# Quad 0, the identity taps and layer 3's rows in the prologue of a four-layer conditioned residual kernel

## The reference

```python
x = x + conv1d(x, W0, K=9, groups=4, pad=4) + (c @ cw.T)[:, :, None] + fside[None, :, None]
for n in (1, 2, 3):
    h = gelu(c @ W0n + b0n); h = gelu(h @ W1n + b1n)
    att = softmax(h @ W2n + b2n)                     # 8 experts per sample
    agg_w = einsum('bk,koi->boi', att, Wn)           # a 64x64 matrix per sample
    agg_b = att @ bias_kn
    x = x + einsum('boi,bih->boh', agg_w, x) + agg_b[:, :, None]
```

## Time and profile before

| | |
|---|---|
| median of 3 runs | 321.65 us (321.52 to 324.29) |
| the profiled execution | 323.18 us, its span 321.3 us |
| PE busy | 309.9 us, 96% of the span |
| DVE busy | 262.4 us, 82% |
| ACT busy | 228.2 us, 71% |
| POOL busy | 129.4 us, 40% |
| DMA | 104.53 MB, 325 GB/s over the span |

### The profile page before, as it was taken

The page is one execution under the profiler, slowest core; times in us unless marked ns, Lnnn a source line. Parts: engine busy times, 40 slices in busy tenths (PEclk is TensorE's granted clock), DMA queues, the critical chain, the costliest instruction groups (busy, mean ns, idle before and its releaser), DMA issues.

```text
span 321.3 us, 6082 instructions
## 1 busy us (share of the span) xinstructions
PE 309.9 (96%) x1474; PEld 251.8 (78%) x1474; DVE 262.4 (82%) x290; ACT 228.2 (71%) x346; POOL 129.4 (40%) x271
## 2 busy tenths in 40 slices
PE   8787999999999999999999999999999999999993
PEld 8556878888888888888888888888888888888872
DVE  5664788889887889888889888898888888987883
ACT  5544677777777788776777777887777777778663
POOL 5510397454444333444433444434444333344400
PEclk9998899999999999999999999999999999999999
DMA  7787366999999999899999999999999999996687
GB/s 230 218 234 281 134 222 212 370 365 364 348 340 342 372 337 373 337 365 360 363 380 340 354 341 359 340 373 336 361 370 353 370 344 368 344 363 280 266 329 274
DMA packets 30946, 104.53 MB, mean 325 GB/s; under 512 B 3428, under 2 KB 4708, under 8 KB 23113
## 3 DMA queue, kind: packets, MB, share of 16 engines
q1 hardware_dynamic: 30938, 104.43, 88.0%
HBM read 36.26 MB, written 33.55 MB: 217 GB/s over the span
## 4 chain that ended last, share of the span: by engine, by line
PE 91%; DMA 3%; SPq 2%; ACT 1%; DVE 1%; issue 0%; DVEq 0%
PE bank L409 54%; PE bank L451 9%; PE bank L453 9%; PE bank L452 9%; PE bank L417 4%; DMA x_sb<-in_x 3%; PE bank L537 2%; SPq L283 2%; PE bank L459 1%; ACT x_hi L628 1%; PE bank L508 1%; PE bank L465 0%; DVE att L837 0%; PE bank L475 0%; PE bank L485 0%
## 5 line engine op out<-in xcount | busy, mean ns | idle before, releaser
L635 ACT ACTIVATE conv_sb<-bank 128x512 f32<-128x512 f32 x128 | 76.2, 596 | 62.9 <-PE bank L409 59.0
L355 POOL COPY a_diag<-table 64x64 f32 (+1 forms) x128 | 49.7, 388 | 132.2 <-PE bank L417 112.6
L762 DVE TENSOR_TENSOR x_lo<-x_sb,x_hi 128x2064 fp32r<-128x2064 f32 x31 | 71.5, 2308 | 24.5 <-ACT x_hi L628 23.3
L365 POOL COPY a_dup<-table 64x128 f32 (+1 forms) x128 | 70.9, 554 | 34.4 <-ACT table L680 16.9
L409 PE MATMUL bank<-x_hi,toep_hi 128*128 128x512 f32 x256 | 84.3, 411 | 0.1
L409 PE MATMUL bank<-x_lo,toep_hi 128*128 128x512 f32 x256 | 80.7, 397 | 0.0
L409 PE MATMUL bank<-x_hi,toep_lo 128*128 128x512 f32 x256 | 80.5, 395 | 0.0
L779 DVE TENSOR_TENSOR ybuf<-ybuf 128x1024 fp32r<-128x1024 f32 x62 | 77.1, 1244 | 1.1
L628 ACT ACTIVATE x_hi<-x_sb 128x2064 fp32r<-128x2064 f32 x32 | 61.7, 1928 | 11.3 <-DMA x_sb<-in_x 11.0
L655 ACT ACTIVATE out_sb<-bank,beta 128x512 f32<-128x512 f32 x93 | 63.4, 684 | 5.0 <-DMA out<-out_sb 1.8
L409 PEld LDWEIGHTS bank<-x_hi,toep_lo 128*128 128x128 f32 x256 | 48.3, 189 | 12.1
(11 more groups left out here) (95 smaller groups left out, 167.0 us busy)
## 6 DMA issues: line engine op xcount, KB each, us to landing
x_sb<-in_x SPq DMA_DIRECT2D x32, 1032.0 KB, 7.8
ybuf<-conv_sb SPq DMA_DIRECT2D x128, 256.0 KB, 5.0
out<-out_sb SPq DMA_DIRECT2D x29, 1024.0 KB, 7.9
out<-out_sb SPq DMA_DIRECT2D x8, 256.0 KB, 2.5
out_sb<-conv_sb SPq DMA_DIRECT2D x8, 128.0 KB
out<-x_sb SPq DMA_DIRECT2D x4, 256.0 KB, 3.4
x_sb<-in_toep SPq DMA_DIRECT2D x1, 640.0 KB, 6.1
early<-in_mixrow SPq DMA_DIRECT2D x1, 390.0 KB
```

The costliest lines, as they stand in the source:

```text
L355: nc.gpsimd.tensor_copy(a3_diag[rows, par, :, C * h + NH * e:C * h + NH * e + NH], table[0][C * e:C * e + C, here, h, :]).then_inc(comp_in, 1)
L365: nc.gpsimd.tensor_copy(a21_dup[rows, par, :, :, NH * e:NH * e + NH], table[1][C * e:C * e + C, here, h, :].unsqueeze(2).to_broadcast([C, ...
L635: nc.scalar.activation(conv_sb[:, par, g, :], conv_ps[g % banks][:, :], ACT.Copy).then_inc(conv_out, 1)
L762: nc.vector.tensor_tensor(x_lo[:, par].rearrange("p g s j -> p (g s j)"), x_sb[:, par].rearrange("p g s j -> p (g s j)"), x_hi[:, par].rea ...
```

## The change

The identity is added only in the columns where it isn't zero, in two instructions (for each of the two tap offsets d, the half of the phase columns that it occupies). Quad 0 is loaded in two transfers, and its high part is made in two instructions and its low part in three. ScalarE issues the four transfers of layer 3's rows, ahead of its first GELU. The first bias product moves behind two groups of the convolution of quad 0, the first bias transpose behind table bank 8, and the orders of ScalarE and VectorE are rewritten around them.

```diff
@@ SP @@
-            sp.wait_ge(rows3_zero, 1)
-            for i in range(RT):
-                n = C * C // RT
-                sp.dma_start(mrow[0][32 * i:32 * i + K + 1], own_h[0:K + 1, n * i:n * i + n]).then_inc(rows3_in, 16)
-            load(0, 0)
+            n = G // 2 * S * JX
+            sp.dma_start(x_sb[:, 0, 0:G // 2]..., x_h[0:128, 0:n]).then_inc(x0_first, 16)
+            sp.dma_start(x_sb[:, 0, G // 2:]..., x_h[0:128, n:]).then_inc(x_in[0], 16)
@@ GpSimd @@
-            nc.gpsimd.tensor_tensor(taps, taps, eyes.to_broadcast([128, 2, G, 128]), ALU.add).then_inc(toep_set, 1)
+            taps, eyes = (t.rearrange("p d g (m h) -> p d g m h", h=QP) for t in
+                          (taps, eye_tap.rearrange("p (d o m) -> p d o m", d=2, o=1)))
+            for d in range(2):
+                h = slice(QP // 2 * d, QP // 2 * d + QP // 2)
+                nc.gpsimd.tensor_tensor(taps[:, d, :, :, h], taps[:, d, :, :, h],
+                                        eyes[:, d, :, :, h].to_broadcast([128, G, 2 * CG, QP // 2]), ALU.add).then_inc(toep_set, 1)
@@ TensorE @@
-            bias_products(0)
             pe.wait_ge(toep_hi_set, 1)
             pe.wait_ge(toep_lo_set, 1)
             taken(BANKS.index(0))
             conv(0, 0, 0, banks=2)
             taken(BANKS.index(1))
+            pe.wait_ge(xlo_first, 2)
+            conv(0, 0, 1, banks=2)
+            bias_products(0)
+            pe.wait_ge(xhi_set, 1)
             pe.wait_ge(xlo_set, 1)
-            for g in range(1, G):
-                conv(0, 0, g, banks=2)
+            conv(0, 0, 2, banks=2)
+            conv(0, 0, 3, banks=2)
+            tables(8)
             bias_turn(0)
-            for t in (8, 9, 10):
-                tables(t)
+            tables(9)
+            tables(10)
             bias_products(1)
@@ ScalarE @@
+            act.wait_ge(rows3_zero, 1)
+            for i in range(RT):
+                n = C * C // RT
+                nc.scalar.dma_start(mrow[0][32 * i:32 * i + K + 1], own_h[0:K + 1, n * i:n * i + n]).then_inc(rows3_in, 16)
             for n in range(NL):
                 act.wait_ge(hid1_ps, n + 1)
...
-            act.wait_ge(toep_set, 1)
+            act.wait_ge(toep_set, 2)
...
-            x_high(0, 0, 0)
-            for t in ACT_TAKES:
-                if t < TG:
-                    table_bank(t)
+            for there, g, done in ((x0_first, slice(0, G // 2), xhi_first), (x_in[0], slice(G // 2, G), xhi_set)):
+                act.wait_ge(there, 16)
+                nc.scalar.activation(x_hi[:, 0, g], x_sb[:, 0, g], ACT.Copy).then_inc(done, 1)
+            table_bank(0)
             conv_copy(0, 0, 0, 0, banks=2)
+            table_bank(2)
             conv_copy(0, 0, 0, 1, banks=2)
+            table_bank(4)
+            table_bank(6)
             conv_copy(0, 0, 0, 2, banks=2)
-            x_high(1, 0, 1)
-            vcol_copy(0)
             conv_copy(0, 0, 0, 3, banks=2)
             table_bank(8)
+            vcol_copy(0)
+            x_high(1, 0, 1)
@@ VectorE @@
             table_bank(3)
+            dve.wait_ge(xhi_first, 1)
+            x_low_part(slice(0, 1)).then_inc(xlo_first, 1)
+            x_low_part(slice(1, 2)).then_inc(xlo_first, 1)
             table_bank(5)
             dve.wait_ge(xhi_set, 1)
-            for g, done in ((slice(0, 1), xlo_first), (slice(1, G), xlo_set)):
-                nc.vector.tensor_tensor(x_lo[:, 0, g], ...).then_inc(done, 1)
+            x_low_part(slice(2, G)).then_inc(xlo_set, 1)
             table_bank(7)
             bias_sum(0)
-            x_low(1, 1)
             table_bank(9)
             bias_sum(1)
             table_bank(11)
+            x_low(1, 1)
             table_bank(13)
             table_bank(15)
             bias_sum(2)
             x_low(2, 0)
             y_low(0, 0, 0)
+            mix_low(0, 0)
             y_low(0, 0, 1)
-            mix_low(0, 0)
```

More of the change, by code:

```diff
@@ L189, in cond_resid_kernel @@
         x_in = [sem("x_in0"), sem("x_in1")]
+        x0_first, xhi_first = sem("x0_first"), sem("xhi_first")
         stored = [sem("stored0"), sem("stored1")]
@@ L266, in _ @@
             sp.dma_start(ident[:], kept_h).then_inc(kept_in, 16)
-            sp.wait_ge(rows3_zero, 1)
-            for i in range(RT):
-                n = C * C // RT
-                sp.dma_start(mrow[0][32 * i:32 * i + K + 1], own_h[0:K + 1, n * i:n * i + n]).then_inc(rows3_in, 16)
-            load(0, 0)
+            n = G // 2 * S * JX
+            sp.dma_start(x_sb[:, 0, 0:G // 2].rearrange("p g s j -> p (g s j)"), x_h[0:128, 0:n]).then_inc(x0_first, 16)
+            sp.dma_start(x_sb[:, 0, G // 2:].rearrange("p g s j -> p (g s j)"), x_h[0:128, n:]).then_inc(x_in[0], 16)
             sp.dma_start(mixrow, mixrow_h).then_inc(mixrow_in, 16)
@@ L375, in _ @@
             taps = toep.rearrange("p (d g m) -> p d g m", d=2, g=G)
-            eyes = eye_tap.rearrange("p (d o m) -> p d o m", d=2, o=1)
-            nc.gpsimd.tensor_tensor(taps, taps, eyes.to_broadcast([128, 2, G, 128]), ALU.add).then_inc(toep_set, 1)
+            taps, eyes = (t.rearrange("p d g (m h) -> p d g m h", h=QP) for t in
[4 more added lines that the diff above has]
+                                        eyes[:, d, :, :, h].to_broadcast([128, G, 2 * CG, QP // 2]), ALU.add).then_inc(toep_set, 1)
             pool.wait_ge(toep_hi_set, 1)
@@ L402, in conv @@
                 if g == 0:
-                    pe.wait_ge(xhi_set, q + 1)
+                    pe.wait_ge(*((xhi_first, 1) if isinstance(q, int) and q == 0 else (xhi_set, q + 1)))
                     pe.wait_ge(*((xlo_first, 1) if isinstance(q, int) and q == 0 else (xlo_set, q + 1)))
@@ L859, in _, with x_low_part @@
             table_bank(3)
+            def x_low_part(g):
+                return nc.vector.tensor_tensor(x_lo[:, 0, g], x_sb[:, 0, g], x_hi[:, 0, g].bitcast(F32), ALU.subtract)
+            dve.wait_ge(xhi_first, 1)
+            x_low_part(slice(0, 1)).then_inc(xlo_first, 1)
+            x_low_part(slice(1, 2)).then_inc(xlo_first, 1)
             table_bank(5)
             dve.wait_ge(xhi_set, 1)
-            for g, done in ((slice(0, 1), xlo_first), (slice(1, G), xlo_set)):
-                nc.vector.tensor_tensor(x_lo[:, 0, g], x_sb[:, 0, g], x_hi[:, 0, g].bitcast(F32),
-                                        ALU.subtract).then_inc(done, 1)
+            x_low_part(slice(2, G)).then_inc(xlo_set, 1)
             table_bank(7)
             bias_sum(0)
-            x_low(1, 1)
             table_bank(9)
```

## The result

The changed kernel takes 317.69 us (median of 4 runs, 317.10 to 318.25), the kernel before 322.33 us (321.52 to 324.29). The ratio is 0.9861, with a 95% interval of 0.9825 to 0.9897: 1.4% faster. The profiled execution took 318.25 us, with a span of 316.4 us.

A forecast was written before the change was run, and what follows sets the result against it. TensorE was taken as the bound, with 91% of the chain. 1.43 + 1.37 + 0.3 + 0.34 - 0.11 = 3.3 us, taken as 3.0 off the median 321.65: about 318.7 us, range 317.8 to 320.9.

The forecast's parts named there:

- (a): First bias product moved behind the first convolution's second group, before 24.70 us: worth nothing while the rows are awaited.
- (b): Quad 0 in two transfers and parts: first convolution at about 15.5 instead of 16.96 us, gain becoming idle time.
- (d): Layer 3's four transfers on ScalarE's queue: GELUs 0.5 us late, net 0.2, more than repaid by (c).
- (c): Identity in half the columns on POOL: adds 1.2 to 1.5 us instead of 2.35, att some 0.6 us earlier.
- (e): TensorE's restart at the copied rows' landing, 24.70 us: follows the backlog of bytes, not the issue; 0.3 us earlier.
- if the restart is not near 24.4: Sign that the prediction is wrong: TensorE's wait for the copied rows does not end near 24.4 us.
- (f): ScalarE's vcol copy ahead of quad 1's x_high: TensorE's 1.43 us wait at the second bias product goes.
- (g): Table matmuls after the second bias product: with TensorE dense, the clock's fall goes too, 1.37 us gained.
- (h): First mix: one y_low moved behind mix_low on VectorE, gaining the 0.34 us wait for mix_lo.
- B: Clock still falls ahead of the tables, which pay 1.37 us: gain 1.9, time 319.7 to 320.4; chance 0.25.
- C: Transfers decide: copied rows land at 25.2 or later, or quad 1's x_lo is awaited; 320.2 to 321.2; chance 0.12.
- D: ScalarE's four issues delay the first GELU: gain eaten at 1.3 us each, 322.6 us at 1.5; chance 0.06.

The follow-up runs named there:

- experiment 3: The changed kernel with layer 3's four row transfers back on SP's queue, ahead of quad 0: 317.86 us, ratio 0.9875.
- experiment 5: The changed kernel with quad 0 loaded in one transfer and its high part made in one instruction: 318.35 us, ratio 0.9881.
- experiment 8: The changed kernel with both VectorE orders undone (x_low(1) ahead of table bank 9 and bias_sum(1), both y_low ahead of mix_low): 323.45 us, ratio 1.0015.
- experiment 11: The changed kernel with only x_low(1) put back ahead of table bank 9 and bias_sum(1): 322.24 us, ratio 0.9987.
- experiment 12: The changed kernel with only both y_low put back ahead of the first mix_low: 318.67 us, ratio 0.9909.
- experiment 4: The changed kernel with POOL's add of the identity in one instruction over all columns: 318.99 us, ratio 0.9908.
- experiment 2: The changed kernel with ScalarE's x_high(1) and vcol_copy(0) back ahead of the last conv_copy of quad 0: 319.11 us, ratio 0.992.
- experiment 7: The kernel before with unread products filling TensorE's two idle pieces, ahead of table 8 and bias_products(1): 322.63 us, ratio 1.0035.
- experiment 10: The kernel before with x_low(1) behind bias_sum(1) on VectorE and vcol_copy(0) ahead of x_high(1) on ScalarE: 319.59 us, ratio 0.9909.
- experiment 6: The kernel before with only ScalarE's last conv_copy of quad 0, vcol_copy(0) and table bank 8 put ahead of x_high(1): 323.79 us, ratio 1.0048.
- experiment 9: The kernel before with only VectorE's x_low(1) moved behind bias_sum(1) and table bank 11: 321.81 us, ratio 0.9998.
- experiment 1: The changed kernel again with no edit, as yardstick: 317.65 us, ratio 0.9865.

## Why the prediction was nearly right, and where it was not

The direction and the place were right: the gain is made before the first mix and arrives whole. The size was low. Forecast 3.0 us off the median, measured 4.6; 317.69 lies 0.1 us below the low end of the range (317.8), and "faster by more than 1%", which I gave 0.24, is what came. Point by point:

- (a), (b), (d): hidden ahead of table 8, as forecast. Experiment 3 shows it for layer 3's rows (0.2 us, with the first GELU at 4.73 where I had 4.7). For quad 0's halves experiment 5 is inconclusive between 0 and 0.7 us. The first convolution came at 17.07 and not at 15.5, since in that execution the clock had fallen at the pair products; it came at 15.38 to 15.76 in experiments 8, 11 and 12, whose profiles have no such stretch, and at 14.82 in experiment 3.
- (c): the adds took 1.64 us against my 1.2 to 1.5, and att came 0.9 us earlier against 0.6. That it did not carry on to the landing is shown by experiments 3 and 4. That undoing the edit costs 1.3 us in the median I had not foreseen, and the cause is open.
- (e): I took 24.4 for the restart, and it was 23.66 and 23.05 in the two profiles of the changed kernel. By my own sign, "if the restart is not near 24.4", the prediction failed here. The idle piece of about 2 us that was to end there was absent in both; in experiments 2 to 5, 8, 11 and 12 it was 0.32 to 1.62 us. The term of 0.3 us for the landing stands against 1.04 us in the two profiles compared. That the landing doesn't follow the issue held: in the changed kernel the copies were issued 0.66 us later and consumed 1.0 us earlier. But table 8 began anywhere from 22.51 to 26.76 over the profiles, in kernels of both sorts, so one profile of each doesn't tell how much of it is the change's. Table 8 began at 23.6 us on average in the four kernels of before's sort (without experiment 7, where work was added) and at 23.5 in the nine of the changed sort, so an earlier start is not shown. What is left of the gain once the path is taken off, 4.6 - 3.8 = 0.8 us, would lie here; but this takes a path of one execution from a difference of medians, and it stays open.
- (f) and (g) together: I had 1.43 + 1.37 = 2.8 us, and experiment 10 measured 2.6 (its path 2.8). The sum was right and its two terms were not. The 1.43 us of waiting for vcol are worth nothing alone (experiment 6), and the 1.37 of slow clock are worth 0.4 by the path (experiment 7), because one step behind both stood bias_turn(1), for which VectorE would have been late anyway. I had seen this for executions without the slow clock ("it lacks only 0.6 us") but booked x_low's new place as a margin and not as a term, while it is the edit without which the others are lost: a path 4.56 us longer in experiment 11. The other margin that I booked, 0.5 us for quad 1's x_lo, was 0.1: it was out at 32.54 and conv(1) began at 32.63. And the slow clock is not given back by TensorE being dense only; in experiments 6 and 11 it fell behind the single wait at bias_turn(1), where it costs in full.
- (h), the step that failed in size: 0.34 us for the order of y_low and mix_low, measured 1.0 (path 1.24) in experiment 12. I priced the idle time that the old chain showed. With everything ahead shortened, TensorE comes to the first mix sooner by more than VectorE does, and in experiments 9 and 10 the wait there has grown to 0.97 us. From the restart to conv(1) the changed kernel needs 9.08 us where I had 9.8: three banks back to back take 2.68 us in the chain; the 2.94 of the earlier trace rows has the start behind an idle piece in it. Experiment 10 keeps the same pace up to conv(1) (8.87 us in the timeline, 8.98 in experiment 1) and gives 0.97 us back at the first mix.
- Rivals: B did not come in its place (no profile of a kernel with x_low late and vcol early has a slow clock behind table 8); C and D not at all. D's deciding price, 1.3 us for an issue by ScalarE, was 0.42. The Trainium skill's figure of 2.66 us for a table switch (ScalarE: Activation LUTs, What ACT_TABLE_LOAD costs) is contradicted once more: the load began at 3.43 and the GELU at 4.73.

By paths, then, the change is: two orders that only work together, 2.8 us, and the order of mix_low, 1.0 to 1.2 us. The rest of the 4.6 us is open. One candidate that I had priced as hidden is (c): the long att of experiments 7 and 10, with TensorE's idle piece, the slow clock and the slow banks behind it, reaches table 8 through TensorE's own work and not through the copied rows. Experiment 4 does not test it, since there att was over before the long add began.

## What to carry to other kernels

An idle piece in the chain is worth its length only up to the next wait for the same event. Here quad 1's landing fed two: ScalarE's x_high with vcol behind it, and VectorE's x_low with bias_sum behind it. Look for everything that stands behind a late transfer in each engine's order, and move all of it in one edit, since moving one can even lose time. After a gain, recompute the small waits downstream from the new arrival times rather than from the old trace.

## What the runs showed of the hardware

- A slow stretch of TensorE's clock cost by what stood behind it: 0.4 us of 1.37 in before, where VectorE was late anyway, and in full in experiments 6 and 11. Late ones, between 30 and 38 us, stood in the profiles of before and of experiments 6, 8 and 11: all of them kernels in which TensorE waits, or would have waited, for bias_turn(1) behind x_low(1). None of the other ten profiles has one there. In experiments 6, 8 and 11 it came behind an idle piece of 2.87, 2.64 and 2.65 us. Pieces of 1.33 to 1.62 us (experiments 2, 3, 8 and 9, at other places) were not followed by a slow stretch; in before two pieces of 1.49 and 1.43 us close together were. Early ones came in experiments 7 and 10 behind idle pieces of 2.17 and 2.08 us, from about 13 to 16.5 us. At the pair products, from about 8 us, they stood in the profiles of the changed kernel and of experiments 1, 2, 4 and 6, where TensorE had stood for at most 0.53 us since its first matmul; what brought these about is open.
- The time from the issue of SP's eight copies to the start of table 8 was 9.7 to 12.7 us over the profiles, for the same 1 MB. Issued at 11.97 (experiment 3) or at 13.13 (experiment 1), the rows were used at 23.07 and 23.05.
- DVE's att, of 24 elements, took 0.18 us when POOL's add had not begun (experiment 4), 0.54 beside two adds of 0.82 us, and 1.42 beside one of 2.35. In twelve of the fourteen profiles it began while an add was running and ended 0.04 to 0.07 us behind that add: it took 1.04 to 2.29 us beside one long add (five profiles) and 0.18 to 0.81 beside two short ones (seven), which let it in between. This agrees with what the Trainium skill says of the shared interface (GPSIMD Engine Reference, Specifications).
